# ScalarE's groups of eight addresses, read at the ends of other places

## The reference

```python
h = jnp.einsum('ni,hid->nhd', layernorm(x), W)
e = leaky(einsum(h[src], a_src) + einsum(h[dst], a_dst))      # slope 0.2
alpha = jnp.exp(e - segment_max(e, dst)[dst])
out_h = segment_sum(alpha / segment_sum(alpha)[dst] * h[src], dst)
x = x + out_h.reshape(N, H * D) @ W_out
t = layernorm(x)
p, i = top_k(softmax(t @ router_w.T), 2)                      # p normed to sum 1
y = sum(combine[:, e] * (gelu(t @ w1[e] + b1[e]) @ w2[e] + b2[e]) for e in experts)
x = x + t + y
```

## Time and profile before

| | |
|---|---|
| median of three runs | 1604.75 us (1602.48 to 1605.58) |
| profiled execution, its own time | 1604.37 us |
| span of that profile | 1602.6 us |
| TensorE busy | 1447.0 us (90%) |
| VectorE busy | 1098.8 us (69%) |
| ScalarE busy | 981.0 us (61%) |
| GpSimd busy | 829.2 us (52%) |
| mean granted TensorE clock | 0.955 |

### The profile page before, as it was taken

How to read it: one execution, slowest core, us unless ns; L and a number is a source line. 1 busy time by engine, 2 the same in 40 slices (tenths; PEclk the granted TensorE clock), 3 DMA queues, 4 the chain that set the end, 5 groups by cost and what they waited for, 6 DMA issues and landing times.

```text
span 1602.6 us, 29587 instructions
## 1 busy us (share of the span) xinstructions
PE 1447.0 (90%) x7327; PEld 1147.4 (72%) x7327; DVE 1098.8 (69%) x3031; ACT 981.0 (61%) x2505; POOL 829.2 (52%) x886
## 2 busy tenths in 40 slices
PE   5916776999999999999999999999999999999998
PEld 3813444777777777777777777777777878787887
DVE  6636665767777777767777777777776767677543
ACT  3705553666667575766666666666675767667632
POOL 1357777555555555555555555555564655551000
PEclk9966786899999999999999999999999999999999
DMA  9565644333343434343334334333334343464000
GB/s 220 141 189 141 179 134 132 102 104 109 106 116 96 118 100 114 105 116 105 114 103 110 109 108 112 109 109 100 117 102 119 96 124 92 123 91 63 1 17 17
DMA packets 89788, 174.83 MB, mean 109 GB/s; under 512 B 22455, under 2 KB 56049, under 8 KB 89593
## 3 DMA queue, kind: packets, MB, share of 16 engines
q0 software_dynamic: 40448, 111.89, 27.4%
q1 hardware_dynamic: 48071, 60.77, 12.7%
q10 hardware_dynamic: 1106, 0.27, 0.1%
HBM read 159.24 MB, written 14.43 MB: 108 GB/s over the span
## 4 chain that ended last, share of the span: by engine, by line
PE 72%; issue 8%; DVE 7%; ACT 4%; POOL 2%; ACTq 1%; DMA 0%; DVEq 0%; POOLq 0%
PE agg_ps L1113 23%; PE ob L1183 18%; PE hb L1137 15%; PE kbank L1073 4%; PE ob L1214 3%; POOL ring L740 2%; PE ob L1137 2%; PE ob L1249 2%; ACT acc L1326 2%; PE ob L1189 1%; DVE ring L848 1%; PE kbank L1089 1%; PE kbank L1081 1%; ACT agg_ps L1329 1%; ACT hT L1358 1%
## 5 line engine op out<-in xcount | busy, mean ns | idle before, releaser
L740 POOL DMA_INDIRECT ring<-table,srcE x832 | 796.9, 958 | 569.5 <-PE agg_ps L1113 330.4
L1113 PE MATMUL agg_ps<-ring,oh 128*128 128x260 f32 x1664 | 558.0, 427 | 27.8 <-ACT agg_ps L1329 16.3
L1326 ACT COPY acc<-agg_ps x831 | 307.8, 370 | 208.8 <-PE agg_ps L1113 151.9
L1183 PE MATMUL ob<-w_sb,hT 128*125 128x256 f32 x1600 | 408.9, 381 | 1.6
L1329 ACT COPY agg_ps<-zc 128x260 f32 x832 | 314.6, 378 | 98.6 <-ACT acc L1326 3.2
L1113 PEld LDWEIGHTS agg_ps<-ring,oh 128*128 128x128 f32 x1664 | 291.4, 199 | 94.4 <-issue 66.0
L1183 PEld LDWEIGHTS ob<-w_sb,hT 128*125 128x125 f32 x1600 | 296.4, 188 | 53.0 <-issue 9.6
L848 DVE TENSOR_TENSOR ring<-ring,kbank 128x1024 f32<-128x1024 f32 x208 | 244.8, 1214 | 50.2 <-ACT ring L1348 50.0
L1358 ACT ACTIVATE hT<-hb,b_sb 128x375 f32<-128x375 f32 (+1 forms) x272 | 154.0, 566 | 169.0 <-PE hb L1137 168.0
L785 DVE TENSOR_TENSOR oh<-kbank,relE 128x512 f32<-128x512 f32 x208 | 141.6, 681 | 126.5 <-PE kbank L1073 124.3
L983 DVE SCALAR_TENSOR_TENSOR y<-ob,cmb,y 125x256 f32<-125x256 f32 x400 | 188.9, 475 | 47.3 <-PE ob L1183 43.7
(11 more groups left out here) (271 smaller groups left out, 1376.7 us busy)
## 6 DMA issues: line engine op xcount, KB each, us to landing
OT<-relb_d SPq DMA_DIRECT2D x52, 512.0 KB
ring<-table,srcE POOLq DMA_INDIRECT x832
y<-in_x_dram SPq DMA_DIRECT2D x50, 125.0 KB
out_dram<-y SPq DMA_DIRECT2D x50, 125.0 KB
table<-hrow SPq DMA_DIRECT2D x25, 227.5 KB
acc<-in_x_dram SPq DMA_DIRECT2D x2, 1568.0 KB
acc<-in_L_ffn_w_dram SPq DMA_DIRECT2D x1, 2048.0 KB, 11.0
w_sb<-in_L_ffn_w_dram SPq DMA_DIRECT2D x1, 2048.0 KB
```

Source lines behind the costliest of these rows:

```text
L740: pool.indirect_dma_start(out=rings[b % RING][:, k, :], out_offset=None, in_=table[:, :], in_offset=bass.IndirectOffsetOnAxis(ap=srcE[:, t ...
L1113: T.matmul(aggf[:, bass.ds(half["at"][k % 8], ROW)], oh[:, (4 * b + q) % OHQ, k % 4, :], rings[b % RING][:, k, :], start=False, stop=True, ...
L1183: t = T.matmul(o[0:Q, 0:D], hT[:, e % 2, f, cols], w2_sb[:, e, f, :], start=f == 0, stop=f == KC - 1)
L1326: A.copy(accf[:, bass.ds(row_of[h][k % 8], ROW)], aggf[:, bass.ds(closed[h][k % 8], ROW)]).then_inc(S["ev"], 1)
```

## The change

The condition that chooses the batch and half turns from `k < 8` to `k < 7`, the wait for the table's arrival moves from place 11 to 7, and the six reads move. For the second half of the running batch: coming bank from 3 to 3, row from 5 to 1, closed bank from 7 to 5. For the first half of the next batch: row from 11 to 7, coming bank from 13 to 8, closed bank from 15 to 12. As sets of places, 3, 5 and 7 hold a read in both kernels, reads at 11, 13 and 15 are gone, and reads at 1, 8 and 12 are new.

```diff
-                        b, h = (it, 1) if k < 8 else (it + 1, 0)
+                        b, h = (it, 1) if k < 7 else (it + 1, 0)
                         if not 0 <= b < NBAT:
                             return
                         part = slice(8 * h, 8 * h + 8)
-                        if k == 11:
+                        if k == 7:
                             act.wait_ge(fld[b % RING], fetched(b))
-                        if k in (5, 11):
+                        if k in (1, 7):
                             row_of[h] = loads(ENG.Activation, tabs[0:1, b % 3, 3, part], (NB - 1) * ROW)
-                        elif k in (3, 13):
+                        elif k in (3, 8):
                             coming[h] = loads(ENG.Activation, tabs[0:1, b % 3, 1, part], (AB - 1) * 512)
-                        elif k in (7, 15):
+                        elif k in (5, 12):
                             closed[h] = loads(ENG.Activation, tabs[0:1, b % 3, 4, part], (AB - 1) * 512)
```

## The result

The changed kernel took 1609.24 us (median of 10 runs, 1608.03 to 1614.84), the kernel before 1604.27 us (10 runs, 1602.48 to 1605.86). The ratio is 1.0037, 95% interval 1.0027 to 1.0047: slower by 5.0 us by the medians and 5.9 by the ratio, outside the predicted range, where 0.8 us less was forecast. The profiled execution of the changed kernel took 1609.3 us, with a span of 1607.5 us.

A forecast was written before the change was run, and what follows sets the result against it. TensorE (busy 90%, 72% of the chain) was taken as the bound. Eleven groups at +0.07 (+0.8 us) and four at -0.40 (-1.6) made -0.8 us: 1603.9 us predicted, 8-in-10 range 1598.2 to 1608.0.

The forecast's parts named there:

- the second batch of the eleven usual groups: Batches 7 to 39: +0.28 us from later exps at TensorE's turn, less waits of 0.16 and 0.23, giving -0.11.
- rival C: Second batch doesn't make good its delay, VectorE bounding TensorE: +0.28 for -0.11, total +3.5, 1608.2 us; chance 8%.
- The 0.23 us: Second batch, TensorE's idle time put down to the gelu of place 14; expected to shrink to nothing.
- The 0.16 us before tile 14's weight load: Second batch, TensorE's wait for the clearing of place 13; expected to shrink to nothing.
- First batches: Eleven usual groups: the read at place 8 makes place 10's clearing and TensorE's tile 12 later, +0.28 us each.
- Third batches: Eleven usual groups: +0.44 at place 8, -0.45 at 11, 0.07 to 0.08 won at 13; rescale earlier, -0.10 us each.
- The last four groups: First batches: earlier clearing, rescale and products, -0.40 us each, -1.6 in all; second and third batches 0.
- The prices of a read: ScalarE read of addresses: 0.44 us bare, 0.28 behind a waiting activation, 0.07 behind an unblocked one, 0 behind a table load.
- Rival A: The read at place 12 isn't hidden behind the gelu's table load: total +4.2, 1609.0 us; chance 12%.
- Rival B: The read at place 8 costs 0.07 us, like behind an unblocked activation: total -6.5, 1598.3 us; chance 20%.
- The wait for the table at place 7: Moved from place 11; the table has landed by then, as TensorE used it at places 0 and 1: cost nothing.

The follow-up runs named there:

- the version with 9: Changed kernel with the read of place 8 moved to 9 in all batches: 1597.81 us, 0.9958 of the kernel before; on a 1740 chip 1.0068 and 1.0057.
- the kernel with 13 at 8: The kernel before with only the read of place 13 moved to place 8: 1617.64 us, ratio 1.0093.
- the first half alone: The kernel before with only the running batch's reads moved, to 1, 3 and 5, and 11, 13, 15 kept: 1604.25 us, ratio 0.9999.

## Why the prediction was wrong

**The step that failed** is the second batch of the eleven usual groups, "0.28 - 0.16 - 0.23 = -0.11": the forecast took two waits of TensorE as time that ScalarE's gain would win back. Measured: +0.28, nothing won back. This is rival C by its effect, 11 x 0.39 = +4.3 us, which the forecast had priced at 1608.2 us with 8%. Three things were wrong in it.

- The 0.23 us were read as a wait for the gelu because the row names it. It was TensorE's own read, which takes 0.59 us and ends 0.02 us ahead of the weight load. The code tells it too: the hidden product waits for the gelu two before its own (L1147), the last reader of the bank that it writes, and that one was long over; and TensorE's read (L1100) stands right there.
- The 0.16 us before tile 14's weight load did vanish, but a weight load is not the matmul: 0.11 us of it reached the matmuls behind, and these are lost at the turn's second part, which waits for VectorE's split (0.15 before, 0.27 in the version with 9).
- The delay of the messages goes on to that split (L927) and from there to the turn's second part. Rival C named VectorE but not this wait.

**First batches** were right in kind and a little small: +0.28 forecast, +0.34 measured, with 0.05 of it at place 2. That is not the read at 1: the kernel with 13 at 8 has most of it (0.03) without that read, and the first half alone, which has the read, moves by less than 0.01. What makes it is open. **Third batches** were right: -0.10 forecast, -0.15 measured.

**The last four groups** were over-sized, and reached another way: -0.40 each forecast, all of it in first batches; about -0.27 measured, half of it in second batches. In the first of them, VectorE's rescale no longer waits for the clearing and the products start without idle matmul time, where 0.72 and 0.42 us had stood:

```profile
1232.41 0.30 PEld L1113 LDWEIGHTS agg_ps<-ring,oh 128*128 128x128 f32 x2 [0.35 <-issue]
...
1233.36 0.42 DVE L841 TENSOR_TENSOR agg_ps<-agg_ps,sc 128x260 f32 x1
...
1235.26 1.02 PE L1073 MATMUL kbank<-d,OT 128*128 x8
```

In the median tile 12 is 0.28 later, tile 15 0.13 earlier than before, and the products at place 1 another 0.41 earlier: 0.54 in all, more than the forecast had. Behind the messages at the end of the second batch 0.27 of it are left. The forecast put the second batch at 0, because it ends on VectorE's own work. But VectorE's work moves with the exps: the version with 9 gains 0.44 in the first and 0.39 in the second batch, and each of the two reads at 8 takes some 0.3 of that back.

The sum of what was measured: 11 x (0.34 + 0.28 - 0.15) = +5.2, less 4 x 0.27 = 1.1, makes +4.1 us. The measured ratio is 5.9 us (4.3 to 7.5). The 1.8 us between are about what one more low-clock stretch at 1.5 us makes, which was in no step of the forecast. That is argued from the profiles and in part only: in the second timing of both kernels on one chip the mean granted clock is 0.9525 over 6 runs of the changed kernel and 0.9531 over 17 of the one before. A stretch takes 0.001 off it (an estimate: half the clock for 3.4 of some 1607 us), so less than one more is seen there, at a ratio of 1.0038. The rest stays open.

**The prices of a read** held: 0.44 bare, 0.28 behind an activation that had waited, nothing behind a table load. Rival A is refuted by the rows of the second batch above: the gelu of place 12 starts at 844.25, right behind the table load, and the next copy at 844.72, 0.47 us later, with the read between them. The trace shows why it costs nothing (line 654, ScalarE, 842.5 to 843.4 us):

```profile
L654 ACTq TENSOR_LOAD <-tabs x1: 544/544/544, 842.7 to 842.7; - x1
```

The sequencer has done the read by 843.24, while the engine is in the table load until 844.23.

Rival B (0.07 at place 8) is refuted by the 0.76 us in the first batch. The Trainium skill's page "ScalarE: Activation LUTs" (What ACT_TABLE_LOAD costs) adds a drain to each table switch; the gelu 0.02 us behind the load's end shows none here, as before. By the Trainium skill's page "Runtime: NRT & Kernel Launch" (Instruction fetch mechanics), at some 200 ns a register, moving one read of eight out of the way would be worth an estimated 1.6 us a batch; against the changed kernel the version with 9 gained 0.28 to 0.44, a read of eight takes 0.55 us in the trace, and the measurement decides.

**What the forecast did not see** is that the same price is paid or not within one place. At 8 the read stands on the way to the exps and to the clearings of 10 to 13. One place later it stands behind a table load and is free. The wait for the table at place 7, costed at nothing, did cost nothing that shows: the version with 9 keeps it. The forecast had both prices in its rows and did not ask what 9 would give.

## What to carry to other kernels

A small operation on an engine that is not the bound costs what stands behind it until that engine next waits. Price each place by what covers it (a table load, an activation that waits) and by who waits for the run of work it heads; here one place was worth 12 us. Before counting a wait as recoverable, ask whether its named releaser had already been done (here 0.25 us), and whether the waiting engine has an instruction of its own there that the timeline does not list; and follow the delay through every engine that it passes, not through the first only.

## What the runs showed of the hardware

- A read of eight addresses takes 0.55 us on ScalarE's sequencer and 0.59 us on TensorE's (medians of 312 and 208 in the kernel before). On TensorE's queue it shows as idle time of the weight load with another engine or "issue" as its releaser: 0.43 and 0.46 us in the rows shown, gone when the read moves.
- A read of eight addresses behind exp's table load and its 0.2 us activation is free on ScalarE (first and second batches within 0.02 us of the kernel before), as behind a gelu's table load (the next copy 0.47 us behind the gelu, 0.48 without a read).
- The granted clock fell to 1.2 GHz for 3.4 us at a time, 19 times of 22 in a third batch behind eight-column matmuls, at about 1.5 us a time. Which batch it hits differs from run to run of one kernel.
- One kernel, two kinds of chip (two chips of each): 1604 and 1731 to 1744 us, and a ratio of 0.9958 on the one against 1.0057 and 1.0068 on the other for the same edit. Between 340 us and the last 20 us the profiles of the second kind hold 48 to 89 us at the lower clock, those of the first 3 to 14.
